# Expert stages of a four-part transformer block: GpSimd's scatters of second choices and fetches of first choices in groups of four, one group for each finished list

## The reference, cut to what matters

```python
probs = softmax(xf @ gate_w.T)             # xf: 4096 normalized tokens, 128 values; 8 experts
top_p, top_i = top_k(probs, 2)             # a first and a second choice for each token
w = top_p / (sum(top_p) + 1e-9)
keep = my_rank < 640                       # the first 640 tokens of each (choice, expert) list
for e in range(8):
    y = (silu(xf @ gate_proj_w[e].T) * (xf @ up_proj_w[e].T)) @ down_proj_w[e].T
    out += comb[:, e:e+1] * y              # comb: w * keep, placed by expert
```

## Time and profile before

| what | value |
|---|---|
| three runs | 1851.42, 1852.36, 1852.57 us; median 1852.36 |
| the profiled execution's own time | 1852.19 us |
| its span | 1850.4 us |
| busy: PE, DVE, ACT, POOL | 67%, 52%, 36%, 29% of the span |
| mean granted share of TensorE's clock | 0.80 |

### The profile page before, as it was taken

One profiled execution on the slowest core, in us unless ns is written; L12 is line 12 of the kernel. 1 busy time (PEld: TensorE's weight loads), 2 busy tenths in 40 slices (PEclk: granted clock), 3 DMA queues, 4 the chain that ended last, 5 costly groups with the idle time before them and its releaser, 6 DMA issues. The chain is left out here.

```text
span 1850.4 us, 26960 instructions
## 1 busy us (share of the span) xinstructions
PE 1232.3 (67%) x9406; PEld 837.2 (45%) x9406; DVE 954.8 (52%) x2142; ACT 659.6 (36%) x1085; POOL 535.2 (29%) x593
## 2 busy tenths in 40 slices
PE   4616968779531392703799998998999984139370
PEld 2414947658331392702244444444444433129370
DVE  5864565556253041415776665776667715304141
ACT  4632222212100151301166654765666660015130
POOL 2424030030436506164024003302400003650616
PEclk9656988889555596855799998999999995559695
DMA  1349011110122232131000010001001002123213
GB/s 43 148 176 406 5 34 57 34 57 0 34 71 66 64 109 67 54 88 40 12 23 3 13 41 8 7 7 48 7 7 30 7 1 67 57 74 101 74 55 89
DMA packets 111650, 105.50 MB, mean 57 GB/s; under 512 B 9264, under 2 KB 95664, under 8 KB 110640
## 3 DMA queue, kind: packets, MB, share of 16 engines
q1 hardware_dynamic: 100224, 85.63, 14.4%
q0 software_dynamic: 8192, 16.79, 3.2%
q10 hardware_dynamic: 3120, 1.57, 0.3%
HBM read 49.17 MB, written 50.59 MB: 54 GB/s over the span
## 5 line engine op out<-in xcount | busy, mean ns | idle before, releaser
L1815 DVE TENSOR_REDUCE att_mx<-att_ps 128x1 f32<-128x512 f32 (+3 forms) x608 | 383.0, 659 | 160.0 <-PE att_ps L1705 115.6
L1583 ACT ACTIVATE att_prob<-att_ps 128x1024 f32<-128x1024 f32 (+3 forms) x384 | 297.6, 810 | 206.4 <-PE att_ps L1717 145.4
L1702 PE MATMUL att_ps<-att_kT,att_q1T 128*128 128x512 bf16 (+3 forms) x768 | 238.9, 341 | 33.3 <-DVE att_mx L1815 11.8
L968 POOL DMA_INDIRECT moe_fetched<-results,moe_fetch_i x128 | 129.4, 1011 | 245.7 <-DMA results<-moe_ys 207.9
L1234 DVE TENSOR_TENSOR moe_hid<-moe_gated,moe_ps_u 128x256 f32<-128x256 f32 (+1 forms) x128 | 62.1, 485 | 260.5 <-ACT moe_gated L1012 169.5
L1714 PE MATMUL att_ps<-att_q2T,att_kT 128*128 128x512 bf16 (+3 forms) x768 | 193.5, 328 | 1.8 <-ACT att_prob L1583 1.2
L1728 PE MATMUL att_pso<-att_prob,att_v 128*32 128x512 f32 (+3 forms) x1536 | 164.9, 502 | 0.0
L1702 PEld LDWEIGHTS att_ps<-att_kT,att_q1T 128*128 128x128 bf16 x768 | 74.4, 98 | 199.3 <-DVE att_mx L1815 143.8
L961 POOL DMA_INDIRECT slots<-moe_rows,moe_place_i x128 | 123.2, 963 | 78.5 <-DVE moe_place_i L1197 41.3
L1079 PE MATMUL moe_ps_g<-moe_xT_hi,expert_wg_hi 128*128 128x256 f32 (+1 forms) x128 | 49.2, 385 | 124.4 <-issue 74.2
L1478 POOL CAST att_qm_rows<-att_nm 128x32 bf16<-128x32 f32 x48 | 15.6, 325 | 371.7 <-DVE att_nm L1824 367.5
(11 more groups left out here) (274 smaller groups left out, 2503.4 us busy)
## 6 DMA issues: line engine op xcount, KB each, us to landing
slots<-fw_zeros SPq DMA_DIRECT2D x2, 5120.0 KB, 28.2
moe_xs<-slots SPq DMA_DIRECT2D x32, 320.0 KB
tok<-prep_tok SPq DMA_DIRECT2D x4, 1536.0 KB, 5.4
turned<-prep_tT SPq DMA_DIRECT2D x4, 1536.0 KB, 8.7
fw_tok<-tok SPq DMA_DIRECT2D x4, 1536.0 KB, 10.4
results<-moe_ys SPq DMA_DIRECT2D x32, 192.0 KB, 2.0
fw_Tkv<-turned SPq DMA_DIRECT2D x4, 1024.0 KB, 6.8
moe_xb<-x SPq DMA_DIRECT2D x8, 512.0 KB, 5.2
```

The source lines that it names most:

```text
L968: pool.indirect_dma_start(fetched[k][:, b * tiles + j], None, results[k], bass.IndirectOffsetOnAxis(ap=fetch_i[b][:, j, k:k + 1], axis=0)) ...
L1583: nc.scalar.activation(prob[(2 * n + pair) % 4][:, :, 0:size], ps2[pair][:, :, 0:size], ACT.Exp, scale=SCORE_SCALE).then_inc(exp_done, 1)
L1702: last = nc.tensor.matmul(out, q1T[t % 2][:, j * P:(j + 1) * P], kT[t][h + k][:, 512 * c:512 * c + size], start=True, stop=not diagonal)
L1815: nc.vector.reduce_max(mx[:, c, j, h:h + g], ps1[unit % 2][:, 0:g * size].rearrange("p (g n) -> p g n", g=g), AX.X).then_inc(max_done, 1)
```

## The change

Two waits are added to POOL's program, for both expert stages. The 32 scatters of second choices and the 32 fetches of first choices are each taken as eight groups of four (g = 2 * b + j // 4). Group 0 has no new wait. Group g of the scatters waits until g lists are finished (`y_done` at 2g). Group g of the fetches waits until 8 + g lists are finished. The scatters of first choices, the fetches of second choices and all other engines' programs stay as they are.

```diff
@@ -958,6 +958,8 @@
                     if k == 0:
                         pool.wait_ge(placed, b + 1)
                     for j in range(tiles):
+                        if k == 1 and j % 4 == 0 and 2 * b + j // 4 >= 1:
+                            pool.wait_ge(y_done, (2 * b + j // 4) * PER)
                         pool.indirect_dma_start(slots, bass.IndirectOffsetOnAxis(ap=place_i[b][:, j, k:k + 1], axis=0), rows[:, b * tiles + j], None).then_inc(slots_written[k], 16)
 
             for k in range(2):
@@ -965,6 +967,8 @@
                     pool.wait_ge(y_stored[s], (k + 1) * (EXPERTS // Y_RING) * PER * 16)
                 for b in range(quarters):
                     for j in range(tiles):
+                        if k == 0 and j % 4 == 0 and 2 * b + j // 4 >= 1:
+                            pool.wait_ge(y_done, (EXPERTS + 2 * b + j // 4) * PER)
                         pool.indirect_dma_start(fetched[k][:, b * tiles + j], None, results[k], bass.IndirectOffsetOnAxis(ap=fetch_i[b][:, j, k:k + 1], axis=0)).then_inc(fetches[k][b], 16)
```

## The result

The changed kernel takes 1764.02 us, the median of four executions (1760.34 to 1764.26), against 1852.46 us (1851.42 to 1853.17) for the kernel before. The ratio is 0.9518, with an interval of 0.9502 to 0.9535: 4.8% faster, some 88 us. The forecast was 1782 us (1731 to 1854), so its direction and its range held, and the gain was larger than its 70.8 us.

What follows compares the result with a forecast made beforehand. Bursts of indirect DMAs on POOL were taken to freeze PE's work, some 72 us a stage; 8.4 + 12.2 + 14.4 + 1.6 = 36.6 us would remain, gaining 35.4 a stage, 70.8 in two: 1852.2 to 1782 us, range 1731 to 1854.

Steps and rivals of the forecast that it cites:

- list 0 without a freeze: First list of a stage, PE's work not almost stood still by back-to-back indirect DMAs: 13 us, from 10 to 20.
- groups 1 to 6 of scatters: Behind lists 0 to 5: each group of four freezes PE for 1.4 us, 8.4 us a stage.
- standstill and clock, list 7: Before list 8's first transpose: PE stands 9.9 us for the last scatters' load, clock restart 2.3 more, together 12.2.
- burst of eight fetches, list 9: Fetch groups 0 and 1 run as one burst: PE frozen 6.4 us, perhaps 1 us of clock.
- groups 2 to 6 of fetches: After the first eight fetches: five groups at 1.4 us each, 7.0 us a stage.
- group 7, list 15: Last fetch group, begun when list 14 ends: costs 0, as PE has only 3.2 us of work left.
- the end behind list 15: DVE's sums meet fetch group 7, so the first fetch of second choices ends 1.6 us later (bounds 0 and 4).
- Rival D: Freezes have another cause, such as cold start and SP's transfers, and stay: 1880 us, 5%.
- rival A: The forecast itself: short bursts cost little, 0.7 to 2.5 us a group, 1766 to 1806 us, 47%.
- rival C: Groups of four cost nothing: 1751 us, or 1731 if burst of eight and restart are free too; 22%.
- Rival B: PE is frozen through every group however short, 6.05 us each: slower, 1893 us, 13%.
- Rival E: Every small freeze also drops the clock to 1.2 GHz and costs 2.3 us: 1833 us, 8%.

Runs made afterwards that it cites:

- the kernel of pairs: Kernel before with waits for scatters and fetches in groups of two, one for each finished block: 1739.66 us, ratio 0.9381.
- the scatters moved ahead: Changed kernel with eight scatters at once, then groups of four released one list and one block earlier: 1745.75 us, ratio 0.9405 against the kernel before.
- the fastest version: Kernel before with scatters six at once, then twos by `gu_done`; fetches three at once, then twos, five at the end: 1721.43 us, ratio 0.927.
- the last two spread versions: Kernel before with scatters released by `gu_done` and spread evenly, fetches in twos with four threes, or without threes: 1732.65 and 1721.43 us.
- the one with threes: Kernel before with scatters six at once, then twos by `gu_done`; fetches in twos and, four times, threes: 1732.65 us, ratio 0.9345.

## Why the prediction was right, step by step

| term of the sum, us in a stage | forecast | measured, stage 1 / 2 | how it is worked out |
|---|---|---|---|
| list 0 without a freeze | 13 | 13.05 / 13.99 | rows above |
| lost before | 72 | 72.4 / 70.7 | the kernel before: list 0 less the row above, lists 9 and 10 less 6.32 each |
| groups 1 to 6 of scatters | 8.4 | 2.9 / 3.0 | 40.84 and 40.89, less 6 x 6.32 |
| standstill and clock, list 7 | 12.2 | 11.8 / 12.7 | 18.11 and 18.97, less 6.32 |
| burst of eight fetches, list 9 | 7.4 | 3.5 / 4.8 | 9.86 and 11.11, less 6.32 |
| groups 2 to 6 of fetches | 7.0 | 5.6 / 2.4 | 37.19 and 34.02, less 5 x 6.32 |
| group 7, list 15 | 0 | 2.8 / 0.6 | 6.44 and 4.24, less 3.66 |
| the end behind list 15 | 1.6 | -2.0 / -0.7 | 48.3 and 49.5 to the last sum, 50.3 and 50.2 before |
| new cost | 36.6 | 24.6 / 22.8 | sum of the last six |

The gain is 72.4 - 24.6 = 47.8 and 70.7 - 22.8 = 47.9 us. The two stages sum to 95.7. The stretch between them took 796.6 us in this execution against 791.6 before, and the first stage began 1.0 us earlier: 95.7 - 5.0 + 1.0 = 91.7, and the two profiled executions are 1852.19 - 1760.34 = 91.9 us apart. The sum closes.

**What bounds the kernel: right.** The freeze is tied to runs of indirect DMAs (with plain DMAs, or with the scatters left out, list 0 is short), it costs what the stretches said, and list 0 is 13 us without it. Rival D, another cause, is refuted by three kernels, and with it what the Trainium skill's page "SBUF — State Buffer" (Who interferes with whom) would make of this case: that TensorE and ScalarE never wait on another engine. The trace doesn't show whether SBUF has a part in it at all. One detail was wrong: there is no burst of 64 scatters. POOL rests 4.6 to 4.8 us between quarters, and 48 scatters run in a row, 1594.10 to 1654.42 us in the second stage.

**The cost of a group: right in kind, too large in size.** This is the term that was mis-sized most. I took 1.4 us from two onsets, 4.3 and 5.0 us into a burst, and from a resumption 1.3 us after one. Measured were 0.49 us for a group of scatters (2.9 / 6), and 0.5 to 1.1 for one of fetches (2.4 / 5 and 5.6 / 5). On POOL's timeline of the changed kernel two groups stand a list apart, as foretold:

```profile
617.94 0.96 POOL L963 DMA_INDIRECT slots<-moe_rows,moe_place_i  x1 [2.06 <-ACT moe_ys L1006]
...
621.73 0.96 POOL L963 DMA_INDIRECT slots<-moe_rows,moe_place_i  x1 [0.30 <-issue]
624.76 0.96 POOL L963 DMA_INDIRECT slots<-moe_rows,moe_place_i  x1 [2.06 <-ACT moe_ys L1006]
```

Where a group cost more, in the fetches of the first stage, the delay sits at the same place of each list: a silu that comes 1.05 us after its group's last fetch (697.47 + 0.94 = 698.41). ScalarE of the changed kernel:

```profile
696.55 0.49 ACT L1006 ACTIVATE moe_ys<-moe_ps_y 128x384 f32<-128x384 f32 x1 [0.95 <-PE moe_ps_y L1095]
699.46 0.49 ACT L1016 ACTIVATE moe_gated<-moe_ps_g 128x384 f32<-128x384 f32 x1 [2.41 <-PE moe_ps_u L1085]
```

With the measured sizes of all terms the new cost would have been 12.0 and 13.8 us lower. The 1.4 us for a group has 5.5 and 5.4 of that in the scatters and 1.4 and 4.6 in the fetches; the burst of eight has 3.9 and 2.6, the end 3.6 and 2.3. The result lies 2 us below rival A's own range, my forecast's, and between it and rival C's 1751: groups of four are cheaper than I took them to be, and not free. That the whole range held says little, since 1731 to 1854 takes in rivals A, C and E. And 1.4 us was meant for a group of four wherever it begins; the runs of four in the kernel of pairs, in the scatters moved ahead and in the fastest version cost 0 to 0.3 on average. Rival B, 4.6 us a group or more, is out by a factor of nine on the scatters. Rival E is out too: the clock is granted in full (1.00) in lists 1 to 6 and 10 to 14, in spite of a small wait in each.

**The standstill: right, also in its parts.** Timeline of the changed kernel, second stage: group 7's first scatter, its last, SP's load of list 8, PE's `down` before it and the transpose after it.

```profile
1629.67 0.96 POOL L963 DMA_INDIRECT slots<-moe_rows,moe_place_i  x1 [2.04 <-ACT moe_ys L1006]
...
1633.47 0.96 POOL L963 DMA_INDIRECT slots<-moe_rows,moe_place_i  x1 [0.30 <-issue]
...
1635.73 0.36 SPq L918 DMA_DIRECT2D moe_xs<-slots  x1
...
1627.46 1.05 PE L1095 MATMUL moe_ps_y<-expert_wd,moe_hid 128*128 128x128 f32 x8
1639.05 0.90 PE L1072 MATMUL moe_ps_t<-moe_ident,moe_xs 128*128 128x128 f32 x3 [10.54 <-DMA moe_xs<-slots]
```

PE waits 10.54 us, 9.9 forecast. From the fourth scatter to the load are 2.26 us (2.2), from there to the transpose 3.32 (3.0). List 7 fell to 6.3 us in the second stage of the last two spread versions, where the scatters were through earlier, so the load's wait made it, and nothing in list 7 itself. SP's backlog of stores, costed at 0, held no one up: list 8 takes a bare 6.32 us behind it.

**The burst of eight: too dear.** Frozen for 6.4 us and 1 us of clock, I had said; 3.5 and 4.8 were measured, and 4.3 to 8.1 in the kernel with groups of eight. PE gets on with some of its work within a burst of this length. The 6.4 us took the freeze for complete from its onset.

**The end: a collision in one stage, and its price wrong.** POOL and DVE of the changed kernel at the end of the second stage:

```profile
1702.58 1.06 POOL L972 DMA_INDIRECT moe_fetched<-results,moe_fetch_i  x1 [0.30 <-issue]
1703.94 5.20 POOL L972 DMA_INDIRECT moe_fetched<-results,moe_fetch_i  x1 [0.30 <-issue]
1709.45 0.94 POOL L972 DMA_INDIRECT moe_fetched<-results,moe_fetch_i  x1 [0.30 <-issue]
...
1701.95 6.38 DVE L1246 SCALAR_TENSOR_TENSOR moe_xb<-moe_fetched,moe_share,moe_xb 128x128 f32<-128x128 f32 x24
1710.94 2.19 DVE L1246 SCALAR_TENSOR_TENSOR moe_xb<-moe_fetched,moe_share,moe_xb 128x128 f32<-128x128 f32 x8 [2.61 <-DMA moe_fetched<-results,moe_fetch_i]
```

A fetch takes 5.20 us instead of 0.95 beside the sums, until 1709.14, 0.8 us after they end (1701.95 + 6.38 = 1708.33). The fetches of second choices had met the sums before as well, so one collision took the place of another. I had the second fetch of group 7 held until 8.9 us after list 14, and three more DMAs behind it, until 12.7. In the trace the third passed in 1.06 us beside the sums and only the fourth was held, so the first fetch of second choices ended 10.6 us after list 14 (1709.45 + 0.94 - 1699.81), against 11.1 before. In the first stage none of the group was held: its last two fetches, at 725.93 and 727.18 us, took 0.95 and 0.99 us though the sums ran from 725.69 us on. So meeting the sums does not by itself hold a fetch. Which fetch is held isn't shown: in the kernels before and after, the held ones began 2.0 to 6.5 us after the sums did, in the one with threes one began 0.3 us before them. The group 7 that I had called free did cost list 15, 2.8 and 0.6 us.

**What stays open.** By what path the indirect DMAs hold PE's results back: whether the matmuls themselves stand or only the signals of their end are late, no trace shows, since the ends of matmuls are modelled. Loading of instructions isn't it: in the kernel before no packet of an instruction queue moved from 1618 to 1662 us, and PE went on at 1640.88 us all the same. Nor is the onset a time since the burst began. In the second stage of the kernel before POOL had issued with rests of only 0.3 us since 1594.10 us, yet DVE got the last ranks at 1599.61 us, 0.04 us after PE's last matmul for them by its modelled end, and ScalarE the first transposes at 1619.19 us; only the results due from 4.3 us into PE's work on list 0 came late. The two onsets of 4.3 and 5.0 us were read where both engines had just begun to be busy together, and what they count from isn't shown. Nor is it shown why a group of four fetches cost 1.1 us in the first stage and 0.5 in the second of the changed kernel; the kernel with fetch waits alone and the one with the earlier scatters showed 1.1 in both.

## What to carry to other kernels

When an engine's results come late while another engine issues a long run of one kind of instruction, cut the run into the shortest groups that the schedule allows, and put a rest between them that other work fills: here 32 in a row cost 35 us, eight 3.5 to 8.1, seven 3.5, four 0.5 to 1.1 when begun at the end of a list and 0 to 0.3 on average when begun at the end of its first block, and pairs beside lists 1 to 3 nothing. Then look on the timeline whether the groups stay apart: waits on one counter can be fulfilled so close together that groups of two and three run as four, five and seven. Before adding a wait, follow the one consumer that needs the last of the group, for there the change charged 12 us a stage; releasing the groups earlier removed all but 1.5 us of it.

## What the runs showed of the hardware that was not expected

Plain DMAs from the same queue, 32 in a row at 0.53 us each beside PE's lists, cost nothing, and indirect ones of the same tiles froze PE's results. The freeze isn't all or nothing: at 1.26 us from DMA to DMA one list passed in 41.8 us, at 1.44 us three passed in 43.5, and beside pairs, or beside fours begun at the end of a first block, lists took 6.3 to 6.8 us, but for two of 7.2 and 7.3. The number of DMAs in a row doesn't explain the cost alone: the same fours of scatters cost 0.5 us each begun at a list's end and 0.2 begun at the end of a first block, and the fours of fetches 0.5 to 1.1 against 0.1 to 0.3. Why the earlier place is cheaper isn't shown.
